# Attention on eight Trainium2 cores: the score matmuls placed behind the PV matmuls of the same iteration

## What is computed

```python
def _L0_attn_ref(hidden_states, scaling, qkv_w, qkv_b, o_w, o_b):
    qkv = hidden_states @ qkv_w.T + qkv_b
    xq, xk, xv = jnp.split(qkv, [H * D, H * D + KV * D], axis=-1)
    ...
    xq = xq * scale[None, None, None, :]
    xk = jnp.repeat(xk, rep, axis=2)
    xv = jnp.repeat(xv, rep, axis=2)
    scores = jnp.einsum('bqhd,bkhd->bhqk', xq, xk)
    probs = jax.nn.softmax(scores.astype(jnp.float32), axis=-1).astype(xq.dtype)
    out = jnp.einsum('bhqk,bkhd->bqhd', probs, xv)
    out = out.reshape(B, S, H * D)
    return out @ o_w.T + o_b
...
x = _layernorm(x + _L0_attn_ref(x, ...), axis=-1)
x = _layernorm(x + _L0_ffn_ref(x, ...), axis=-1)
```

## Time and profile before

| | us |
|---|---|
| median of 2 runs | 5787.3 (5764.5 to 5810.1) |
| the profiled execution | 5763.5 |
| its span, slowest core (core 7) | 5762.5 |
| spans of the 8 cores | 5732.2 to 5762.5 |
| busy: TensorE matmul / weight load | 4026.8 (70%) / 2468.7 (43%) |
| busy: ScalarE / VectorE / GpSimd | 2458.0 (43%) / 2057.0 (36%) / 126.5 (2%) |
| mean granted TensorE clock | 0.876 |

### The profile page before, as it was taken

One profiled execution on the slowest core, in us unless ns is written; L12 is line 12 of the kernel. 1 busy time (PEld: TensorE's weight loads), 2 busy tenths in 40 slices (PEclk: granted clock), 3 DMA queues, 4 the chain that ended last, 5 costly groups with the idle time before them and its releaser, 6 DMA issues. The chain is left out here.

```text
span 5762.5 us, 81166 instructions; the slowest of 8 cores (5732.2 to 5762.5 us)
## 1 busy us (share of the span) xinstructions
PE 4026.8 (70%) x29508; PEld 2468.7 (43%) x29508; DVE 2057.0 (36%) x2495; ACT 2458.0 (43%) x2360; POOL 126.5 (2%) x125
## 2 busy tenths in 40 slices
PE   2545666666666666666666661499769958995997
PEld 0222222222222222222222220388658847883886
DVE  2011334242343433333324333344434434434444
ACT  0113786868768687676886760000000000000000
POOL 0000101101000000000000000000000000000000
PEclk9767898989889898988998885699879979997998
DMA  2222413314132000100001004221232141222211
GB/s 78 57 50 64 132 56 109 104 38 126 50 93 73 16 22 1 37 1 8 30 1 37 1 8 110 74 89 67 92 92 89 67 139 45 89 89 66 89 67 52
DMA packets 188570, 360.80 MB, mean 63 GB/s; under 512 B 104097, under 2 KB 104097, under 8 KB 171682
## 3 DMA queue, kind: packets, MB, share of 16 engines
q1 hardware_dynamic: 188194, 355.62, 19.3%
HBM read 259.04 MB, written 73.40 MB: 58 GB/s over the span
## 5 line engine op out<-in xcount | busy, mean ns | idle before, releaser
L615 ACT ACTIVATE pb<-psS,consts 128x1024 bf16<-128x1024 f32 x2048 | 2187.5, 1112 | 696.0 <-PE psC L603 424.9
L567 PE MATMUL psS<-QT,KTC 64*128 64x512 bf16 x2048 | 807.1, 395 | 516.3 <-ACT pb L615 507.2
L592 PE MATMUL psC<-pb,Vp 64*128 64x512 bf16 x2048 | 823.6, 402 | 343.9 <-DVE mrgS L505 328.2
L955 ACT ACTIVATE gs<-psS 128x1024 bf16<-128x1024 f32 x160 | 163.8, 1024 | 1591.2 <-PE psS L933 1591.2
L567 PEld LDWEIGHTS psS<-QT,KTC 64*128 64x128 bf16 x2048 | 193.0, 95 | 1505.0 <-issue 1505.0
L571 PE MATMUL psS<-QT,KTC 64*128 64x512 bf16 x2048 | 836.5, 409 | 0.0
L595 PE MATMUL psC<-pb,Vp 64*128 64x512 bf16 x2048 | 830.2, 405 | 0.0
L603 PE MATMUL psC<-pb,Vp 64*128 64x512 bf16 x2048 | 823.4, 402 | 0.0
L599 PE MATMUL psC<-pb,Vp 64*128 64x512 bf16 x2048 | 820.0, 400 | 0.0
L933 PE MATMUL psS<-x1f,ew 128*128 128x256 bf16 x5120 | 600.3, 277 | 190.0 <-DMA x1f<-x1b 141.2
L495 DVE COPY mrgP<-psC 64x512 f32<-64x512 f32 x64 | 43.7, 682 | 1678.1 <-PE psC L603 1678.1
(11 more groups left out here) (109 smaller groups left out, 2717.9 us busy)
## 6 DMA issues: line engine op xcount, KB each, us to landing
ew<-ewb SPq DMA_DIRECT2D x129, 1024.0 KB, 7.3
ewb<-ewcast SPq DMA_DIRECT2D x120, 256.0 KB, 3.2
x0b<-x SPq DMA_DIRECT2D x32, 512.0 KB, 4.0
cstage<-wg SPq DMA_DIRECT2D x32, 512.0 KB, 4.4
cstage<-wu SPq DMA_DIRECT2D x32, 512.0 KB, 4.4
cstage<-wd SPq DMA_DIRECT2D x32, 512.0 KB, 4.2
x0r<-x SPq DMA_DIRECT2D x32, 512.0 KB, 4.5
x1s<-x1t SPq DMA_DIRECT2D x32, 512.0 KB, 3.2
```

The lines of the kernel that those rows point to most:

```text
L567: tn.matmul(psS[0:128, so:so + QC], KTC[kcS][0:64, ko:ko + 128], QT[pS][0:64, q0:q0 + QC], start=True, stop=True, tile_position=(0, 0))
L592: tn.matmul(psC[0:128, 0:QC], Vp[gE][0:64, vo:vo + 128], pb[slp][0:64, 0:QC], start=st, stop=sp, tile_position=(0, 0))
L615: SC.inc(sc.activation(pb[ke % 4][:, 0:2 * QC], psS[:, sl * 1024:sl * 1024 + 2 * QC], AF.Exp, bias=consts[:, CNC:CNC + 1]))
```

## The change

In the loop over v the block that issues the two score matmuls of block v moves, unchanged, from ahead of the PV block to behind it. ScalarE's exp, the waits' targets and all buffers stay as they are. The counts that the waits compare with are those of TensorE's new order.

```diff
             for v in range(NB + 4):
-                if v < NB:
-                    pS, ktS = divmod(v, kt_n)
-                    sl = v % 2
-                    so = sl * 1024
-                    ko = ktS * 128
-                    kcS = pS // rep
-                    SC.wait(tn, b._expslot.get(sl, 0))
-                    tn.matmul(psS[0:128, so:so + QC],
-                              KTC[kcS][0:64, ko:ko + 128],
-                              QT[pS][0:64, q0:q0 + QC],
-                              start=True, stop=True, tile_position=(0, 0))
-                    TN.inc(tn.matmul(psS[0:128, so + QC:so + 2 * QC],
-                                     KTC[kcS][64:128, ko:ko + 128],
-                                     QT[pS][64:128, q0:q0 + QC],
-                                     start=True, stop=True,
-                                     tile_position=(64, 0)))
-                    scores_done[v] = TN.n
                 if v >= 4:
                     u = v - 4
                     pP, ktP = divmod(u, kt_n)
...
                     b._pbslot[slp] = TN.n
                     if sp:
                         pending_fin = (pP, TN.n, pP == 0)
+                if v < NB:
+                    pS, ktS = divmod(v, kt_n)
+                    sl = v % 2
+                    so = sl * 1024
+                    ko = ktS * 128
+                    kcS = pS // rep
+                    SC.wait(tn, b._expslot.get(sl, 0))
+                    tn.matmul(psS[0:128, so:so + QC],
+                              KTC[kcS][0:64, ko:ko + 128],
+                              QT[pS][0:64, q0:q0 + QC],
+                              start=True, stop=True, tile_position=(0, 0))
+                    TN.inc(tn.matmul(psS[0:128, so + QC:so + 2 * QC],
+                                     KTC[kcS][64:128, ko:ko + 128],
+                                     QT[pS][64:128, q0:q0 + QC],
+                                     start=True, stop=True,
+                                     tile_position=(64, 0)))
+                    scores_done[v] = TN.n
                 if 1 <= v <= NB:
                     ke = v - 1
                     sl = ke % 2
```

## The result

| | before | after |
|---|---|---|
| median of all executions | 5831.3 us (10) | 5681.4 us (11) |
| undisturbed executions | 5760.3 to 5812.4 us (5) | 5576.5 to 5583.8 us (5) |
| the profiled execution | 5763.5 us | 5581.7 us |
| its slowest core's span | 5762.5 us | 5580.6 us |

The kernel became faster: the ratio of the undisturbed executions is 0.9649, with a 95% interval of 0.9603 to 0.9694.

A forecast was written before the change was run, and what follows sets the result against it. Attention's steady part was taken as bound by a loop of latencies, neither by ScalarE's rate nor TensorE's. 154 + 57 - 3 = 208 us saved, 5555 us (-3.6%) against 5763.5; range 5525 to 5625.

The forecast's parts named there:

- The loop: Attention's steady part before the edit: exp k, scores k+2, PV k-2, exp k+2 wait in turn, 2.18 us for two exps.
- Steady part: 1768 exp intervals outside crossings and chunk starts: from 1.093 to 1.006 us each, 154 us saved.
- The 1.04 us: ScalarE's exp interval estimated by the skill's rule, 1040 ns; the saving would be about 151 us, the time 5612.
- Crossings: 56 changes of head pair: VectorE starts one exp earlier, four exp intervals take 10.5 us against 11.5; 57 us saved.
- its last sign of being wrong: At a crossing between head pairs: the prediction is wrong if the restart is longer than 10.5.
- the walk: Step-by-step timing of a crossing from exp w-4's start: scores w-2 at 1.25, TensorE restarts at 8.62, exp w at 10.18.
- Starts of chunks: Start of each of 8 chunks: scores 4 now come behind PV 0, which waits for VectorE; 3 us lost.
- the term that leads from one execution to the measured time: Whole kernel: runs lie up to 46 us apart, upward; the median shown lay 24 us above the profiled execution.
- (a): Steady part: ScalarE is slower beside PV than at a chunk's start, interval 1.045; 143 us saved, 5620 us; chance 0.07.
- (b): Steady part: 1.09 us is ScalarE's floor, only crossings gain; 62 us saved, 5701 us; chance 0.08.
- (c): Between crossings: TensorE is granted 1.2 GHz and becomes the bound; 188 us more, 5951 us; chance 0.04.
- (d): Steady part: the edit has no effect, exp v-1 is still held by a PV; 5763.5 us; chance 0.02.

The follow-up runs named there:

- half-width kernels: Kernel before and changed kernel, each with exps on 512 of 1024 columns, the second head's exps left out: steady interval 0.879 us (before), 0.693 us (changed).

## Why the prediction was right, and where not

**The loop was the bound.** Right: cut by the order or by a buffer it gives 1.00, closed again it gives 1.10, and both half-width kernels hit their sums. Two readings carried it. The intervals between starts, taken from merged rows, showed 1.09 beside 1.00 for the same instruction; and one chain of starts and ends closed to 2.18 us without a remainder. The 696 us of idle time on the page would have led to the other answer, since 0.09 us of each wait is hidden by overlapping durations.

**Steady part, -154 forecast, -163 measured.** The interval came out at 1.001, at the lower end of 1.00 to 1.012. The 1.04 us that the prediction worked out as an estimate from the Trainium skill ("ScalarE: Activation LUTs", section "What ACT_TABLE_LOAD costs") don't hold for this exp: the trace shows 1.00 from start to start.

**Crossings, -57 forecast, -28 measured.** This term was mis-sized: a crossing gained 0.50 us, where the forecast was 1.01 and its own bounds 0.6 to 1.4. By its last sign of being wrong, "if a crossing's restart is longer than 10.5", the prediction failed here: the four intervals take 11.0. VectorE does start one exp earlier, and the walk holds where it can be laid on the trace: scores w-2 at 1038.80, the restart at 1046.16, 7.36 us later (forecast 8.62 - 1.25 = 7.37). What was too small, by the means over 56 crossings:
- the interval to exp w, 7.41 against 7.16. Exps recorded back to back grow longer in this kernel (exp w-4 takes 1.27 us), so scores w-2, which wait for its end, start 1.41 us behind its start and not 1.25; and I took 0.10 where the earlier trace rows had already shown 0.16 behind scores.
- the next three, 1.29, 1.20 and 1.12 against 1.23, 1.09 and 1.01. Three pairs of matmuls at 1.2 GHz take 1.28, not 1.23 (the 0.80 of the earlier trace rows is the faster beginning of a burst), and the low clock isn't over after 3.6 us everywhere: at the crossing below it lasts from 1046.16 to 1051.66, and exp w+2 and w+3 still come at 1.28. Over the 56 crossings it lasts from 2.7 to 6.1 us, with a median of 4.4. I took its length from one window. With the clock kept up these intervals are 1.01, 1.00 and 1.00, which shows the cause; that was measured with scores w ahead of PV w-4.

TensorE's timeline at that crossing:

```profile
1046.16 0.58 PE L575 MATMUL psC<-pb,Vp 64*128 64x512 bf16 x1 [5.97 <-DVE mrgS L505]
...
1050.81 0.63 PE L600 MATMUL psS<-QT,KTC 64*128 64x512 bf16 x1
...
1051.66 0.46 PE L582 MATMUL psC<-pb,Vp 64*128 64x512 bf16 x1
...
1051.97 0.38 PE L600 MATMUL psS<-QT,KTC 64*128 64x512 bf16 x1
```

**Starts of chunks, +3 forecast, +2.5 measured.** Right.

**The time.** By the profiled executions the sum gave 5555 and the chip 5582, inside the range; the steady part gained 9 us more than forecast and the crossings 29 us less. The ratio was forecast as 0.964 and came out as 0.965, and that is luck: by the profiled executions it is 0.968, and 0.965 comes from the two longer executions of before. The median of all eleven executions, 5681, lies outside 5525 to 5625. The step that failed is the term that leads from one execution to the measured time: "runs of one kernel lie up to 46 us apart, upward", drawn from two executions of before, whose median lay 24 us above the profiled one. Of the eleven, five lie within 7 us of each other (5576 to 5584) and six 105 to 329 us above the fastest, so the median stands 100 us above the profiled execution. What parts the two groups stays open. With one more execution in the lower group the median would have been 5584, inside the range; the ten executions of the kernel before spread likewise, from 5760 to 6159 us.

**The rivals.** (a) and (b) fell with the interval of 1.001. (c) fell: the clock over the whole of attention is 0.89 in both kernels, and in the 30 us from 1054 on, between two crossings, it is 0.98. (d) fell with the interval too, and at a crossing the exps wait for scores, as forecast, 6.11 us (forecast about 6.0).

## What to carry to other kernels

A merged row without idle time doesn't prove that the engine is the bound: divide it, compare its pace with the same instruction's where fewer waits apply, and look for a closed chain of starts and ends through the other engine. In a software pipeline the order within an iteration and the number of buffers in the ring can be one and the same knob: here moving scores behind PV, or one buffer more, cut the same loop, and either alone is enough. Where an engine waits for a drain, count the drain's instructions by partitions: here operations over 64 partitions cost as much as those over 128 (0.68 and 0.69 us), and the low clock behind the stall was a second price (1.1 us), which repeated matmuls in the stall saved. For a forecast of a median, one or two executions don't show how far it can lie above them.

## What the runs showed of the hardware

The recorded duration of a back-to-back exp isn't constant. The instructions of the exp's line in the kernel before (min, median, max in ns) and after:

```profile
L615 ACT ACTIVATE pb<-psS,consts x2048: 1096/1114/1123, 543.1 to 3426.1; 128x1024 bf16<-128x1024 f32 x187
...
L615 ACT ACTIVATE pb<-psS,consts x2048: 1095/1181/1314, 546.1 to 3242.1; 128x1024 bf16<-128x1024 f32 x187
```

In the changed kernel the durations grow from exp to exp by some 8 ns, up to 1.31 us, and fall back to 1.11 at the next stall (core 5): starts follow each other every 0.997 us, ends every 1.005, and the difference collects in the durations. I take this from the records; which of the two is the engine's own pace, and what makes the difference, isn't shown.

TensorE's granted clock: after a stall of 6.0 us 20 to 21 matmuls on average run at 1.2 GHz (0.58 to 0.63 us instead of 0.38), after one of 2.8 us 15 to 18 (cores 7 and 5), after one of 1.05 us still 10 to 11 (cores 3 and 0), and with the stall filled none. The averages hide a wide spread within one profile: 12 to 28 at the single crossings after 6.0 us, and after 1.05 us either none (at 15 to 20 of the 56) or 14 to 18.
